# Scaled rows stored per choice in the first mixture feed-forward of a four-layer early-fusion model (1 core)

## The reference, cut to what matters

```python
logits = X @ Wg + bg                      # X: normed tokens
topv, topi = top_k(logits, 2)
w = softmax(topv)                         # one weight per choice
xs = X[:, :, None, :] * w[..., None]      # the row is scaled AHEAD of the expert
out = X
for e in range(8):
    h = silu(xs @ W1[e]) * (xs @ W3[e])   # 256 -> 1024
    y = h @ W2[e]                         # 1024 -> 256
    out = out + where(topi == e, y, 0).sum(choices)
```

## Time and profile before

| | |
|---|---|
| runs | 1627.62 us, median of 3 (1624.96 to 1629.68) |
| profiled execution | 1619.05 us, its span 1617.2 us |
| TensorE (PE) busy | 1522.4 us, 94% |
| VectorE (DVE), ScalarE (ACT), GpSimd (POOL) busy | 49%, 31%, 27% |
| chain that ended last | PE 67%, DVE 12%; DMA, ACT, POOL 1% each |

### The profile page before, as it was taken

How to read it: one execution, slowest core, us unless ns; L and a number is a source line. 1 busy time by engine, 2 the same in 40 slices (tenths; PEclk the granted TensorE clock), 3 DMA queues, 4 the chain that set the end, 5 groups by cost and what they waited for, 6 DMA issues and landing times.

```text
span 1617.2 us, 22240 instructions
## 1 busy us (share of the span) xinstructions
PE 1522.4 (94%) x7946; PEld 1102.0 (68%) x7946; DVE 784.4 (49%) x1691; ACT 503.6 (31%) x1002; POOL 441.1 (27%) x433
## 2 busy tenths in 40 slices
PE   6999989987999999999999999999989998998889
PEld 5543345467999999999996555678864445666763
DVE  3668989973111111111107774013675564887704
ACT  1366555521122122222214522222310005655330
POOL 1457878812111111111114000000010001332272
PEclk9999999998999999999999997999999999999899
DMA  6345444544167465412312002001000001000033
GB/s 192 107 107 151 130 109 128 117 163 169 73 213 250 139 217 192 152 52 79 128 52 72 1 1 75 0 0 53 1 1 1 0 0 53 1 1 20 20 105 114
DMA packets 54181, 139.10 MB, mean 86 GB/s; under 512 B 9356, under 2 KB 33061, under 8 KB 47397
## 3 DMA queue, kind: packets, MB, share of 16 engines
q1 hardware_dynamic: 47492, 121.79, 23.5%
q0 software_dynamic: 5760, 15.74, 3.1%
q10 hardware_dynamic: 816, 0.14, 0.0%
HBM read 202.24 MB, written 14.03 MB: 134 GB/s over the span
## 4 chain that ended last, share of the span: by engine, by line
PE 67%; DVE 12%; issue 1%; ACT 1%; DMA 1%; POOL 1%; DVEq 0%; SPq 0%; ACTq 0%; POOLq 0%
PE psum L823 41%; PE psum L1149 10%; PE psum L855 6%; DVE work L1917 2%; DVE work L2058 2%; PE psum L833 1%; DVE work L2057 1%; PE psum L920 1%; PE psum L1003 1%; DVE bst L1568 1%; PE psum L1189 1%; PE psum L1198 1%; DVE work L2066 1%; DVE sq L1596 1%; PE psum L858 1%
## 5 line engine op out<-in xcount | busy, mean ns | idle before, releaser
L823 PE MATMUL psum<-work 128*128 128x128 f32 (+3 forms) x3400 | 472.9, 301 | 9.3 <-DMA tokb<-in_tokb 9.3
L823 PEld LDWEIGHTS psum<-work 128*128 128x128 f32 x3400 | 442.6, 194 | 26.6 <-DMA tokb<-in_tokb 9.3
L1985 DVE TENSOR_TENSOR work<-sq,psum 128x512 f32<-128x512 f32 x82 | 56.3, 687 | 392.4 <-PE psum L823 392.4
L2111 POOL TENSOR_TENSOR rs<-rs,power 128x4 f32<-128x4 f32 (+3 forms) x40 | 44.6, 1116 | 476.2 <-DVE rs L1575 469.9
L2147 POOL TENSOR_TENSOR work<-work,w_late 128x408 f32<-128x408 f32 (+1 forms) x160 | 160.3, 1051 | 38.2 <-DVE work L1917 24.2
L1917 DVE TENSOR_TENSOR_SCAN work<-psum,work 128x414 f32<-128x414 f32 (+1 forms) x160 | 156.8, 1052 | 7.6 <-ACT psum L1361 7.2
L1149 PE MATMUL psum<-w_late,xn 128*128 128x512 f32 x352 | 155.6, 600 | 0.6 <-ACT work L1253 0.6
L920 PE MATMUL psum<-work,xn 128*128 128x408 f32 (+1 forms) x320 | 141.8, 564 | 11.7 <-DVE work L1935 6.5
L2173 POOL DMA_INDIRECT y_rows<-sq,row_of x41 | 40.5, 987 | 363.6 <-ACT sq L1253 363.6
L1361 ACT ACTIVATE psum<-work,a_neg 128x408 f32<-128x408 f32 (+1 forms) x160 | 100.0, 627 | 81.3 <-DVE work L1917 81.3
L1794 DVE SCALAR_TENSOR_TENSOR h<-psum,gate,h 128x256 f32<-128x256 f32 x176 | 76.9, 479 | 99.7 <-PE psum L1149 95.8
(11 more groups left out here) (286 smaller groups left out, 2064.5 us busy)
## 6 DMA issues: line engine op xcount, KB each, us to landing
work<-in_W SPq DMA_DIRECT2D x123, 1024.0 KB
w_attn<-in_unit SPq DMA_DIRECT2D x96, 192.0 KB, 3.0
w_late<-c_rows SPq DMA_DIRECT2D x48, 204.0 KB, 3.2
w_late<-c_rows SPq DMA_DIRECT2D x32, 238.0 KB, 3.7
work<-y_rows SPq DMA_DIRECT2D x11, 512.0 KB, 6.0
work<-in_unit SPq DMA_DIRECT2D x22, 192.0 KB, 5.1
w_late<-in_we SPq DMA_DIRECT2D x2, 2048.0 KB, 8.2
work<-in_xp SPq DMA_DIRECT2D x1, 2700.0 KB, 15.4
```

The lines of the kernel that those rows point to most:

```text
L823: mm = pe.matmul(dst, lhs(k), rhs(k), start=(k == 0), stop=(k == parts - 1))
L1985: dve.tensor_tensor(hm[:, j % 2, 4 * q:4 * q + 4, :].rearrange("p k n -> p (k n)"), sa[:, i % 2], A.at(("e3", j, q)), ALU.mult).then_inc(s ...
```

## The change

The rows are scaled before they are stored, once for each choice, and the map carries numbers only:

- `x_rows` holds 4352 rows. Rows 0 to 2175 are the normed rows times the weight of the first choice, rows 2176 to 4351 those times the weight of the second.
- ScalarE scales, 34 operations of 128x256: for each group first the second choice, out of place into `x2` (a part of the second weight buffer `w13[:, 1]`) or `x2_last`, then the first choice in place in `xtok`. They stand behind the router's exponential. Units 44 and 45 are scaled behind the second group, 46 and 47 behind the last.
- SP makes ten stores instead of five. The loads of units 44 and 45 now stand ahead of them, those of 46 and 47 behind. The weights of block 1 also wait for all stores, since `x2` lies in their buffer.
- POOL's multiply and `weights_placed` are gone; `in_block` has 41 columns a pair instead of 82, and `inv(0)` writes 123 columns (41 three times) instead of 164.
- `slots_of(0)` loses the subtraction of 2176 and the copy of the weights: one operation ahead of `row_of[:, 0]` instead of three.
- `scale_x` is gone; the transposes of a block wait for its gather directly.

```diff
-    x_rows = nc.dram_tensor("x_rows", (TOKENS, D), F32, kind="Internal").ap()
+    x_rows = nc.dram_tensor("x_rows", (SLOTS * TOKENS, D), F32, kind="Internal").ap()
...
-        in_block = work[:, at0[0]:at0[0] + SLOTS * TILES * 2 * BLOCKS].rearrange("p (i a j) -> p i a j", a=2, j=BLOCKS)
+        in_block = work[:, at0[0]:at0[0] + SLOTS * TILES * BLOCKS].rearrange("p (i j) -> p i j", j=BLOCKS)
+        x2 = w13[:, 1].rearrange("p w k n -> p (w k n)").rearrange("p (i n) -> p i n", n=D)
+        x2_last = work[:, at0[0] + SLOTS * TILES * BLOCKS:at0[0] + SLOTS * TILES * BLOCKS + D].rearrange("p (i n) -> p i n", n=D)
+        second = lambda t0, t1: x2[:, t0:t1, :] if t1 < TILES else x2_last
...
@@ SP
-            for t0, t1 in GROUPS:
-                sp.wait_ge(sem("nx"), TILES * L0F + t1)
-                sp.dma_start(x_rows.rearrange("(i p) d -> p i d", p=P)[:, t0:t1, :], xtok[:, 0, t0:t1, :]).then_inc(
-                    sem("x_stored"), 16)
-            for i in range(IN_SCAN + PSLOTS, BRIDGE):
+            for i in range(IN_SCAN + PSLOTS, IN_SCAN + PSLOTS + 2):
+                load_unit(i)
+            for g, (t0, t1) in enumerate(GROUPS):
+                for k in range(SLOTS):
+                    sp.wait_ge(sem("x_scaled"), SLOTS * g + k + 1)
+                    dst = x_rows[(1 - k) * TOKENS:(2 - k) * TOKENS].rearrange("(i p) d -> p i d", p=P)[:, t0:t1, :]
+                    sp.dma_start(dst, xtok[:, 0, t0:t1, :] if k else second(t0, t1)).then_inc(sem("x_stored"), 16)
+            for i in range(IN_SCAN + PSLOTS + 2, BRIDGE):
                 load_unit(i)
             sp.wait_ge(sem("blocks_known"), 1)
+            sp.wait_ge(sem("x_stored"), 16 * SLOTS * len(GROUPS))
             load_w13(1)
             load_w2(1)
...
@@ TensorE, inv and xT_
-                if s == 0:
-                    pe.wait_ge(sem("weights_placed"), 1)
...
-                        wide, n = (2, 6)[s], (2 - s) * blocks
+                        wide, n = (3, 6)[s], blocks
...
-                pe.wait_ge(sem("x_scaled"), j + 1)
+                pe.wait_ge(sem(f"row{j % XR}"), 16 * (j // XR + 1))
...
@@ ScalarE
             router_act(0)
-            for i in range(IN_SCAN + PSLOTS, BRIDGE):
+            act.wait_ge(sem("chosen_weights"), 1)
+            for g, (t0, t1) in enumerate(GROUPS):
+                for k, to in ((1, second(t0, t1)), (0, xtok[:, 0, t0:t1, :])):
+                    for i in range(t0, t1):
+                        ins = act.activation(to[:, i - t0, :], xtok[:, 0, i, :], ACT.Copy, scale=gcol[:, 5 + k, i:i + 1])
+                    ins.then_inc(sem("x_scaled"), 1)
+                if g == 1:
+                    for i in range(IN_SCAN + PSLOTS, IN_SCAN + PSLOTS + 2):
+                        scale_unit(i)
+            for i in range(IN_SCAN + PSLOTS + 2, BRIDGE):
                 scale_unit(i)
             keep_comp(2)
-
-            def scale_x(j):
-                if j == 0:
-                    act.wait_ge(sem("slots_known"), 3)
-                act.wait_ge(sem(f"row{j % XR}"), 16 * (j // XR + 1))
-                act.activation(xblk[:, j % XR], xblk[:, j % XR], ACT.Copy, scale=slot_of[:, 2, j:j + 1]).then_inc(
-                    sem("x_scaled"), 1)
...
@@ VectorE
-                    link(dve.tensor_scalar(late, v, float(TOKENS), float(TOKENS), ALU.is_gt, ALU.mult))
-                    link(dve.scalar_tensor_tensor(src, v, -1.0, late, ALU.add, ALU.subtract))
-                    link(dve.tensor_scalar(src, src, 0.0, None, ALU.max))
+                link(dve.tensor_scalar(src, v, -1.0, 0.0, ALU.add, ALU.max))
...
-                if s == 0:
-                    dve.tensor_copy(slot_of[:, 2], got[:, BLOCKS:2 * BLOCKS]).then_inc(sem("slots_known"), 1)
...
@@ POOL
-            pool.wait_ge(sem("placed"), 1)
-            pool.wait_ge(sem("chosen_weights"), 1)
-            pool.tensor_tensor(in_block[:, :, 1, :], in_block[:, :, 1, :], gcol[:, 5:5 + SLOTS].rearrange(
-                "p s i -> p (s i)").unsqueeze(2).to_broadcast([P, SLOTS * TILES, BLOCKS]), ALU.mult).then_inc(
-                sem("weights_placed"), 1)
...
-            pool.wait_ge(sem("x_stored"), 16 * len(GROUPS))
+            pool.wait_ge(sem("x_stored"), 16 * SLOTS * len(GROUPS))
             pool.wait_ge(sem("slots_known"), 1)
```

More of the change, by code:

```diff
@@ L189, in build @@
         place_i = sb("place_i", [P, SLOTS, TILES], I32)
-        slot_of = sb("slot_of", [P, 3, BLOCKS])
+        slot_of = sb("slot_of", [P, 2, BLOCKS])
         row_of = sb("row_of", [P, 2, BLOCKS], I32)
@@ L273, in build @@
         onehot = xtok[:, 1].rearrange("p i n -> p (i n)").rearrange("p (s i q) -> p s i q", s=SLOTS, i=TILES)
-        in_block = work[:, at0[0]:at0[0] + SLOTS * TILES * 2 * BLOCKS].rearrange("p (i a j) -> p i a j", a=2, j=BLOCKS)
+        in_block = work[:, at0[0]:at0[0] + SLOTS * TILES * BLOCKS].rearrange("p (i j) -> p i j", j=BLOCKS)
+        x2 = w13[:, 1].rearrange("p w k n -> p (w k n)").rearrange("p (i n) -> p i n", n=D)
+        x2_last = work[:, at0[0] + SLOTS * TILES * BLOCKS:at0[0] + SLOTS * TILES * BLOCKS + D].rearrange("p (i n) -> p i n", n=D)
+        assert GROUPS[-1] == (TILES - 1, TILES) and x2.shape[1] == TILES - 1
+        second = lambda t0, t1: x2[:, t0:t1, :] if t1 < TILES else x2_last
         ytok = work[:, 0:SLOTS * TILES * D].rearrange("p (s i n) -> p s i n", s=SLOTS, i=TILES)
@@ L510, in build @@
         plan_units(6)
-        Q.plan(("inv", 0), (sem("slots_known"), 3))
+        Q.plan(("inv", 0), (sem("slots_known"), 2))
         step("inv", 0)
@@ L636, in build @@
                 if b == BATCH:
-                    A.plan(("inv", 1), (sem("slots_known"), 5))
+                    A.plan(("inv", 1), (sem("slots_known"), 4))
                     step("inv", 1)
@@ L778, in _ @@
                 if j == 3:
-                    sp.wait_ge(sem("x_stored"), 16 * len(GROUPS))
+                    sp.wait_ge(sem("x_stored"), 16 * SLOTS * len(GROUPS))
                 if 4 <= j < 4 + PAIRS:
@@ L799, in _ @@
                 sp.wait_ge(sem("nx"), TILES * L3F + (k + 1) * n)
-                sp.dma_start(x_rows.rearrange("(i p) d -> p i d", p=P)[:, k * n:(k + 1) * n, :], xtok3[:, k]).then_inc(
+                sp.dma_start(x_rows[0:TOKENS].rearrange("(i p) d -> p i d", p=P)[:, k * n:(k + 1) * n, :], xtok3[:, k]).then_inc(
                     sem("x_stored"), 16)
@@ L980, in inv @@
                         g = k * tiles + i
-                        hot, rows = ((onehot[:, k, i, :], in_block[:, g].rearrange("p a j -> p (a j)")) if s == 0 else
-                                     (onehot3[:, i, :], in_block3[:, i, :]))
-                        wide, n = (2, 6)[s], (2 - s) * blocks
+                        hot, rows = (onehot[:, k, i, :], in_block[:, g]) if s == 0 else (onehot3[:, i, :], in_block3[:, i, :])
+                        wide, n = (3, 6)[s], blocks
                         mm = pe.matmul(dst[:, 0:wide * n].rearrange("p (r n) -> p r n", n=n), hot,
@@ L1388, in keep_y @@
                 copy(yblk[:, j % 2], B.at(("ey", j))[:, 0:D], "y_kept")
-            scale_x(0)
-            scale_x(1)
             keep_xT(0)
             for j in range(BLOCKS):
-                if j + 2 < BLOCKS:
-                    scale_x(j + 2)
                 if j + 1 < BLOCKS:
@@ L1681, in places @@
                 if s == 0:
[L1682 to L1685, removed]
+                    link(dve.tensor_tensor(in_block, per_block(j_of.rearrange("p s i -> p (s i)")), js, ALU.is_equal))
+                    dve.tensor_tensor(in_block, in_block, per_block(row_id), ALU.mult).then_inc(sem("placed"), 1)
                 else:
@@ L2200, in _ @@
             ln(L3F, range(len(POWER3), len(GROUPS)))
-            pool.wait_ge(sem("x_stored"), 16 * (len(GROUPS) + GROUP))
-            pool.wait_ge(sem("slots_known"), 4)
+            pool.wait_ge(sem("x_stored"), 16 * (SLOTS * len(GROUPS) + GROUP))
+            pool.wait_ge(sem("slots_known"), 3)
             for j in range(BLOCKS3):
@@ L2208, in _ @@
                     row_of[:, 0, j:j + 1], 0)).then_inc(row3(g), 16)
-            pool.wait_ge(sem("slots_known"), 5)
+            pool.wait_ge(sem("slots_known"), 4)
             for j in range(BLOCKS3):
```

2 lines of the change are left out of this document (removed).

## The result

The changed kernel took 1621.57 us, the median of 12 runs (1613.83 to 1625.81), against 1627.51 of 12 runs of the kernel before (1620.37 to 1631.76) on the same chip: ratio 0.9963, 95% interval 0.9946 to 0.9979. That is 5.9 us faster; 7.0 were forecast.

The account below looks back on a forecast made before the run. TensorE's own work bounds the steady blocks, so only the bridge ahead of them matters: 6.5 us from earlier row numbers plus 0.5 from the dropped scaling make 7.0, 1627.62 to 1620.6 us; range 1614.5 to 1627.

Parts of the forecast that it names:

- the earlier row numbers: VectorE's row numbers ahead of the first gather: ready at 377.65 instead of 384.13, first gather 6.5 us earlier.
- The POOL step: POOL's multiply before the inverse map: without it the map starts at 369.5, 2.4 us earlier, at full clock.
- The second gather: Gather ahead of the first block: issued at 380.1, takes 6.3 us in weight traffic, lands at 386.4 and decides the start.
- Rival (a): Second gather lands in 2.7 us; first block 9.8 us earlier, up to 12.3 with the clock; 1616.5 to 1615.3; chance 0.20.
- The stores: Ten stores of scaled rows: 11.6 us at 386 GB/s, paced by ScalarE, last landing 376.3, hidden with 2.2 us to spare.
- Rival (c): Stores become the bound once the last lands after 385.5; slower, 1630.6 us; chance 0.07.
- Units 46 and 47: Weight units loaded behind the stores: there at 377.7 and 380.1, so the first block can't start before about 384.3.
- The first block: First expert block on TensorE: starts at 387.1 instead of 394.06, its 9.55 us left unchanged.
- (b): No change: the gather gets through only when surrounding transfers end; 1627.6 us, or 1624 with half that delay; chance 0.18.

Follow-up runs that it names:

- the wide map: Changed kernel with the map's matmuls back at 164 columns: map lasted 9.79 us, second block at 40.24 us; 1610.77 us in a single run.
- the quiet variant: Changed kernel with SP issuing block 1's and the next layer's weights only after the second gather landed: 1602.66 us, ratio to the kernel before 0.9944.
- the quiet variants: Changed kernel holding weights until the second gather landed, all released together (1602.66 us) or block 1's first weights alone first (1606.79 us, another chip).

## Why the prediction was right

**The step that carries the gain** was the earlier row numbers: forecast 6.5 us, measured 27.06 - 20.84 = 6.2. The map's start was right to 0.2 us and its length to 0.14; the price of 0.111 us for each matmul, taken from the other layer's narrower map, held at 123 columns (7.84 / 68 = 0.115).

**The POOL step** stood in the sum as 2.4 us of wait and 1.6 of clock. In the change it gave 2.3 and 1.5 (13.97 - 11.66, and 11.30 - 9.79 of the wide map); the other 1.95 of the map are the columns. Put back, it cost more: 2.7 and 2.85, because the clock stayed low for longer than in the kernel before (0.50 to 378 there; 0.50 to 374 and 0.73 to 376 in the earlier trace rows).

**The second gather** at 6.3 us in traffic was 6.8. That it was the traffic, as assumed, and not the gather's own time, the quiet variant shows (2.80). Rival (a) priced this: 2.1 us of its 9.8 - 7.0 = 2.8 for the first block were there to be had, and most of the clock's part (block 0 in 7.2 us). But they come only when the weights are held back; in the changed kernel's own order the weights flow beside the gather, against what (a) supposed.

**The stores** were the weak term. I took 386 GB/s for them from the earlier trace rows; they pass at 338 to 341 here, so 4.46 MB need 13.1 us and not 11.6. That is still less than ScalarE's scalings, which ended at 14.5 (14.3 forecast), so the pace was ScalarE's as I had said. The last store was issued 0.3 us later than I had it and landed 4.8 us behind its issue where I had 3.9, and that took half of the slack: about 1 us instead of 2.2. The result hid this, since 1 us of slack is as good as 2.2, but two unit loads ahead of the stores used it up. Rival (c) was far from true all the same: it needed a last landing at 27.5 (385.5 less 357.96), and it came at 19.5. Its 7.0 and 10.0 us of landing did not return; the ten stores took 3.0 to 4.8.

**Units 46 and 47** reached ScalarE at 21.3 and 23.9 us, 1.6 and 1.8 later than forecast (377.7 and 380.1 less 357.96): SP issued the first of them at 16.8, where I had 15.5, and it took 4.6 us to arrive, where I had 4.2. TensorE was done with them at 26.3, and ScalarE's copies at 27.9, still ahead of the gather's 29.2; the quiet variants start at 27.6 for this reason, not at the 26.3 that (a) gave.

**The first block** was put down at 9.55 us as before and took 8.77: the clock fell later. I had counted nothing for this, and it makes up for the gather's half microsecond. That 7.24 stands so near the 7.0 of the sum is therefore in part luck: two sizes were off and cancel, and the first block's start, the date that I had worked out, moved by 6.46.

**The measured time** moved by 5.9 us and, on the other chip, by 2.8 (medians; 4.5 by the ratio), where the bridge says 7.2. Both intervals hold it. Much of their width goes with the granted clock and not with the change: a part that the change doesn't touch lost 5 us to it from one execution to the next, and of the twelve runs of the changed kernel the four with a mean clock of 0.976 or more took 1613.8 to 1618.2 us, the six with 0.972 or less 1620.9 to 1625.7 (the two between, at 0.973, 1617.2 and 1625.8). I can't exclude that part of the bridge's gain is lost in what follows; in the one repeated profile the parts behind it sum to 768.3 against 768.8 before, so nothing was lost there.

**The range** was not worked out as it says. 9.8 us earlier is 1617.8, and 1616.5 lies halfway to (a)'s 1615.3; half of (b)'s delay is 1624. The stated 1614.5 to 1627 is wider than these at both ends, by 2 and 3 us for which the text gives no sum. The result lies inside either way.

## What to carry to other kernels

Follow a bridge between two dense stages from one fixed operation to the next, and judge a change by that distance; a span can hide all of it. An operation of another engine ahead of TensorE costs its wait and, when the clock falls in the idle time, up to as much again (2.3 and 1.5 us here, 2.7 and 2.85 when put back). Holding back 5.6 MB that nobody needed yet shortened a gather from 6.8 to 2.8 us. Of what is held back, the part needed first should then flow alone: that was worth another half microsecond.

## What was not expected of the hardware

- Stores of 1 KB rows from SBUF to DRAM passed at 338 to 341 GB/s with all transfer engines busy in the changed kernel and in the variant with twice the stores, but at 385 to 386 in the kernel before (346 to 350). The difference is not explained. Loads of weights with the gathers among them passed at 410 (the stretch 386 to 388 above).
- ScalarE stood still once for 11.5 us with its input ready, in one of twelve profiled executions.
- The same instructions between layer 2's dense experts and layer 3's gather took 330.4 to 335.7 us in those executions. In the two of the same kernel the 5.4 us between them are two stretches in which TensorE's granted clock was 0.50 in one and not in the other.
